# Near scores by one fp32 product a chunk in the edge attention, spread between the sum groups, and gathers without a pause on POOL

## The reference, cut to what matters

```python
h_all = einsum('nf,rof->rno', x, W).reshape(r, n, h, d)     # 8 relations, 8 heads of 32
h_src = h_all[edge_type, src]                               # one row an edge
h_dst = h_all[edge_type, dst]
scores = einsum('ehd,hd->eh', h_src, attn_src) + einsum('ehd,hd->eh', h_dst, attn_dst)
scores = where(scores > 0, scores, 0.2 * scores)
amax = maximum(segment_max(scores, dst), 0.0)
w = exp(scores - amax[dst])
w = w / (segment_sum(w, dst) + 1e-12)[dst]
out = segment_sum(h_src * w[..., None], dst)
```

## Time and profile before

| what | before |
|---|---|
| time, median of three runs | 4772.35 us |
| the three runs | 4758.54 to 4772.65 us |
| the profiled execution, its own time | 4762.77 us |
| its span on the core | 4761.1 us |
| mean granted clock of PE | 0.827 of 2.4 GHz |
| bytes moved by transfers | 387.91 MB, mean 81 GB/s |

### The profile page before, as it was taken

One profiled execution on the slowest core, in us unless ns is written; L12 is line 12 of the kernel. 1 busy time (PEld: TensorE's weight loads), 2 busy tenths in 40 slices (PEclk: granted clock), 3 DMA queues, 4 the chain that ended last, 5 costly groups with the idle time before them and its releaser, 6 DMA issues. The chain is left out here.

```text
span 4761.1 us, 55035 instructions
## 1 busy us (share of the span) xinstructions
PE 3172.2 (67%) x15106; PEld 2308.6 (48%) x15107; DVE 2073.8 (44%) x4472; ACT 620.2 (13%) x1234; POOL 1288.2 (27%) x2031
## 2 busy tenths in 40 slices
PE   1899799679846317999459512256556665637998
PEld 0666588568735316777334212144344444425555
DVE  6999501310143630000233374365666666732333
ACT  0111100100022102322112100000000000002222
POOL 2700100000010230000300002787878887500000
PEclk9999899889978658999769856577777777857999
DMA  3522244244300012112223103344444444200000
GB/s 105 214 96 96 97 124 131 62 124 124 96 10 0 0 59 76 48 48 84 65 91 150 52 0 57 96 124 116 118 114 125 124 121 119 83 31 20 14 13 27
DMA packets 315432, 387.91 MB, mean 81 GB/s; under 512 B 43120, under 2 KB 259521, under 8 KB 311873
## 3 DMA queue, kind: packets, MB, share of 16 engines
q1 hardware_dynamic: 240642, 222.05, 14.2%
q0 software_dynamic: 49040, 140.22, 10.5%
q10 hardware_dynamic: 25648, 24.42, 1.7%
HBM read 271.43 MB, written 115.17 MB: 81 GB/s over the span
## 5 line engine op out<-in xcount | busy, mean ns | idle before, releaser
L1987 POOL DMA_INDIRECT att_ring<-relation_rows,table_row x784 | 777.3, 991 | 119.9 <-issue 4.7
L2098 PE MATMUL att_acc<-att_ring,att_onehot 128*128 128x264 f32 x1568 | 487.7, 464 | 22.8 <-issue 21.6
L2098 PEld LDWEIGHTS att_acc<-att_ring,att_onehot 128*128 128x128 f32 x1568 | 345.0, 231 | 115.1 <-issue 52.6
L446 PE MATMUL counts_acc<-onehot_lo,onehot_key 128*128 128x400 bf16 x2000 | 362.5, 337 | 43.0 <-DVE onehot_key L428 43.0
L2061 PE MATMUL att_po<-att_near,att_onehotT 128*128 128x64 bf16 x2352 | 147.0, 204 | 315.0 <-issue 263.2
L425 DVE TENSOR_SCALAR onehot_lo<-node_ids,source_lo 128x800 bf16<-128x800 int16 x1000 | 350.4, 416 | 0.0
L446 PEld LDWEIGHTS counts_acc<-onehot_lo,onehot_key 128*128 128x128 bf16 x2000 | 267.9, 139 | 141.7 <-DVE onehot_key L428 82.7
L625 PE MATMUL agg_agg<-x_gnn,agg_slab 128*128 128x257 f32 x1250 | 277.5, 381 | 66.1 <-DMA agg_slab<-edge_counts 66.1
L625 PE MATMUL agg_agg<-xn,agg_slab 128*128 128x257 f32 x1250 | 278.6, 382 | 22.5 <-DMA agg_slab<-edge_counts 22.5
L625 PEld LDWEIGHTS agg_agg<-x_gnn,agg_slab 128*128 128x128 f32 x1250 | 237.9, 190 | 101.9 <-DMA agg_slab<-edge_counts 66.5
L2061 PEld LDWEIGHTS att_po<-att_near,att_onehotT 128*128 128x128 bf16 x2352 | 104.5, 103 | 351.7 <-issue 351.6
(11 more groups left out here) (397 smaller groups left out, 4542.5 us busy)
## 6 DMA issues: line engine op xcount, KB each, us to landing
agg_slab<-edge_counts SPq DMA_DIRECT2D x50, 1600.0 KB, 7.4
edge_counts<-counts_out SPq DMA_DIRECT2D x100, 400.0 KB, 2.4
relation_rows<-tab_out SPq DMA_DIRECT2D x25, 1056.0 KB, 4.0
att_targets<-targets SPq DMA_DIRECT2D x28, 896.0 KB
wide_w<-L_ffn_W ACTq DMA_DIRECT2D x14, 1024.0 KB, 6.9
att_ring<-relation_rows,table_row POOLq DMA_INDIRECT x784
expert_rows_in<-blank_rows POOLq DMA_DIRECT2D x34, 256.0 KB
expert_rows_out<-blank_rows POOLq DMA_DIRECT2D x33, 256.0 KB
```

Source lines behind the costliest of these rows:

```text
L446: mm = nc.tensor.matmul(acc[:, k, h, 0:HALF_LO], oh_key[:, k, :, j], oh_lo[:, k, j, h * HALF_LO:(h + 1) * HALF_LO], start=False, stop=Fals ...
L1987: nc.gpsimd.indirect_dma_start(slots(p)[:, j, :], None, rows_of, bass.IndirectOffsetOnAxis(ap=c.row[:, n:n + 1], axis=0)).then_inc(landed[ ...
L2098: mm = nc.tensor.matmul(acc[:, 0:RW], oh[:, j, :], slots(p)[:, j, :], start=j == 0, stop=False)
```

## The change

- The near scores stay fp32: one piece in place of three in `relation_tables`, its store and `attend`. PE makes one fp32 product a chunk (28 calls a part) in place of three bfloat16 ones.
- These products no longer stand in one block. Group 0 of part p+2 stands after `flip(p+1)` and ahead of the first sum group, group 1 after `to_column(p+1, 0)`, group 2 after `to_column(p+1, 1)`, and groups 3 to 6 where all stood.
- The transposed one-hot is fp32 and is made in two halves: one ahead of the first scan, one after the sum one-hots 5 and 6.
- POOL issues the gathers without the addition and its wait.
- The scores are no longer stored in `attend`; the branch for unsorted edges works them out anew.
- SP's part loads run three parts ahead.

```diff
@@ relation_tables, the drain @@
-                    link(nc.vector.tensor_copy(by_head(near[:, b, 0, :]), own))
-                    link(nc.vector.tensor_tensor(by_head(rest[:, b, :]), own, by_head(near[:, b, 0, :]), ALU.subtract))
-                    link(nc.vector.tensor_copy(near[:, b, 1, :], rest[:, b, :]))
-                    link(nc.vector.tensor_tensor(rest[:, b, :], rest[:, b, :], near[:, b, 1, :], ALU.subtract))
-                    nc.vector.tensor_copy(near[:, b, 2, :], rest[:, b, :]).then_inc(read_v, 1)
+                    nc.vector.tensor_copy(near[:, b, :].rearrange("p (h r) -> p r h", h=HD), own).then_inc(read_v, 1)
@@ attend @@
-        ohT = g.sb(ctx, f"{name}_onehotT", [P, PE_LEN], BF16)
-        near = g.sb(ctx, f"{name}_near", [P, 2, 3, sc], BF16)
+        ohT = g.sb(ctx, f"{name}_onehotT", [P, PE_LEN])
+        near = g.sb(ctx, f"{name}_near", [P, 2, sc])
@@ attend, POOL @@
-                    pl.wait_ge(paused, n + 1)
-                    nc.gpsimd.tensor_tensor(pause, pause, pause, ALU.add).then_inc(paused, 1)
@@ attend, SP @@
                     if p:
-                        sp.wait_ge(ohT_ready, p)
+                        sp.wait_ge(ohT_ready, 2 * p)
...
+                part_loads(2)
                 for p in range(NPART):
-                    if p + 2 < NPART:
-                        part_loads(p + 2)
+                    if p + 3 < NPART:
+                        part_loads(p + 3)
@@ attend, ACT @@
-                    act.wait_ge(st_ready, p + 1)
-                    act.dma_start(kept[p, :, :], st[:, p % 2, :, :, :].rearrange("p c h r -> p (c h r)")
-                                  ).then_inc(st_kept[p % 2], 16)
@@ attend, PE @@
+                def own_scores(p, *groups):
+                    if p >= NPART:
+                        return
+                    for q in groups:
+                        if q == 0:
+                            pe.wait_ge(near_in[p % 2], 16 * (p // 2 + 1))
+                            pe.wait_ge(ohT_ready, 2 * p + 1)
+                            if p:
+                                pe.wait_ge(own_ready, p)
+                        if q == half // MGRP:
+                            pe.wait_ge(ohT_ready, 2 * p + 2)
+                        for j in range(q * MGRP, (q + 1) * MGRP):
                             mm = nc.tensor.matmul(po[:, j // bank, j % bank * sc:(j % bank + 1) * sc],
+                                                  ohT[:, j * P:(j + 1) * P], near[:, p % 2, :], start=True, stop=True)
+                        if q == MG - 1:
+                            mm.then_inc(own_sum, 1)
...
                         flip(p + 1)
+                    own_scores(p + 2, 0)
                     of_this(p, 0)
...
                         to_column(p + 1, 0)
+                    own_scores(p + 2, 1)
                     of_this(p, 2)
...
                         to_column(p + 1, 1)
+                    own_scores(p + 2, 2)
                     of_this(p, 4)
                     if more:
                         flip_back(p + 1)
-                    if p + 2 < NPART:
-                        own_scores(p + 2)
+                    own_scores(p + 2, 3, 4, 5, 6)
                     of_this(p, 5)
@@ attend, DVE @@
-                    nc.vector.tensor_scalar(ohT, tb, lane_a[:, 0:1], None, ALU.is_equal).then_inc(ohT_ready, 1)
+                    part = slice(k * half * P, (k + 1) * half * P)
+                    nc.vector.tensor_scalar(ohT[:, part], tb[:, part], lane_a[:, 0:1], None, ALU.is_equal
+                                            ).then_inc(ohT_ready, 1)
...
-                    if p >= 2:
-                        v.wait_ge(st_kept[p % 2], 16 * (p // 2))
...
                     n = p + 1
+                    if n + 1 < NPART:
+                        targets_of_lanes(n + 1, 0)
                     if n < NPART:
                         v.wait_ge(turned, n + 1)
                         scan_runs(n, 0, ahead, pseq[0:PH, 0:2 * P])
                     onehots(p, 5)
                     onehots(p, 6)
+                    if n + 1 < NPART:
+                        targets_of_lanes(n + 1, 1)
...
-                    if n + 1 < NPART:
-                        targets_of_lanes(n + 1)
                     onehots(n, 1)
```

More of the change, by code:

```diff
@@ L1912, in _, with attend @@
                 link(nc.vector.tensor_copy(c.unsorted, first))
-def attend(g, name, c, gaps, table, near_rows, targets, sums, kept):
+def attend(g, name, c, gaps, table, near_rows, targets, sums):
     nc = g.nc
@@ L1946, in attend @@
         carry = g.sb(ctx, f"{name}_carry", [1, RW])
-        pause = g.sb(ctx, f"{name}_pause", [1, 1], I32)
-        paused = g.sem(f"{name}_paused")
         po = g.ps(ctx, f"{name}_po", [P, 4, MMN])
@@ L1960, in attend @@
         landed = [g.sem(f"{name}_landed{k}") for k in range(RING)]
-        st_kept, near_in = ([g.sem(f"{name}_{n}{k}") for k in range(2)] for n in ("scores_kept", "near_in"))
+        near_in = [g.sem(f"{name}_near_in{k}") for k in range(2)]
         (tb_in, chain_s, st_ready, turned, ends, row_out, into_in, col_out, scanned, back, less_ready, share_ready,
@@ L1979, in _ @@
             def _(pl):
-                nc.gpsimd.memset(pause, 0).then_inc(paused, 1)
                 for n in range(NC):
@@ L2012, in _ @@
                 sp.wait_ge(stored, 16 * NPART)
-                for k in range(2):
-                    sp.wait_ge(st_kept[k], 16 * (NPART // 2))
             @block.scalar
@@ L2112, in nothing @@
                     pass
-                own_scores(0)
+                own_scores(0, *range(MG))
                 for p in range(-1, NPART):
@@ L2260, in onehots @@
                         ALU.is_equal).then_inc(oh_ready, 1)
-                targets_of_lanes(0)
+                targets_of_lanes(0, 0)
+                targets_of_lanes(0, 1)
                 own_scores(0)
@@ L2762, in build_program @@
             g.end_of_stage()
-            attend(g, "att", c, gaps, table, dst_rows, targets, sums, kept)
+            attend(g, "att", c, gaps, table, dst_rows, targets, sums)
         g.end_of_stage()
@@ L2768, in build_program @@
             greatest = g.sb(own, "greatest", [P, NC, HD])
-            late_scores(g, c, kept, scores)
+            late_scores(g, c, table, dst_rows, scores)
             g.end_of_stage()
```

107 lines of the change are left out of this document (63 added, 44 removed).

## The result

The changed kernel takes 4742.2 us (median of 5 runs, 4739.9 to 4749.4) against 4770.2 for the kernel before in 5 runs: a ratio of 0.9956, interval 0.9941 to 0.9971. It is faster by 28 us, where 118 was forecast. The profiled execution took 4744.5 us, 18 less than the profiled one before.

The account below looks back on a forecast made before the run. POOL's gathers were taken as the pace for nine tenths, ring waits for the rest. 42 us (POOL's pace), 75 (ring waits) and 1 (tables' tail) made 118 off 4762.8: 4645 us, range 4575 to 4765.

Parts of the forecast that it names:

- POOL's pace: Gathers in `attend`: without the addition, POOL's floor falls from 1066 to 1024 us, 36.6 a part, 42 us less.
- The disturbance by the fp32 one-hot: Gathers beside DVE's transposed one-hot are stretched; with two fp32 halves this grows from 24 to 40 us.
- the 62 set beside it: By the skill page's lock rule, all of the fp32 one-hot's time would stall POOL: 62 us in place of 40.
- the hold-up: PE's short bfloat16 near products are held up while gathers run; DVE waits about 10.5 us a part for them.
- the 42 of this term: The gain from POOL's pace in `attend`: its floor of 1066 us becomes 1024.
- One bound: DVE's one-hot half in fp32, read from the sum groups' one-hot, 512 elements in 0.67 us: about 2 us.
- Ring waits, 75 us: POOL's waits for a free ring group in `attend` fall from 115 to 40 us; bounds 0 and 115.
- the hold-up stays and is only paid elsewhere: Rival: near products still held up beside gathers, ring waits stay 115, only POOL's 42 us won: 4720 us, chance 0.16.
- The sign that the prediction's last sentence names: In `attend`, DVE's wait moving to the row and column exchanges would show the forecast wrong; no size given.
- Slower: Rival: held-up near products stand ahead of the sum groups, 6.9 us a part more: 4893 or 4851 us, chance 0.13.
- the forecast's own mechanism: In `attend`, hold-up mostly gone and POOL the pace: 4645 us, own range 4565 to 4705, chance 0.62.

Follow-up runs that it names:

- e5: The changed kernel unaltered, on a chip without the hold-up: 4587.5 us, 0.9879 of the kernel before.
- e13: The kernel before without POOL's addition and its wait, transposed one-hot built on ACT in two passes, chip without the hold-up: 4548.6 us, 0.9799.
- e8: The kernel before with only POOL's small addition and its wait taken out, chip without the hold-up: 4569.3 us, 0.9839.
- e6: The changed kernel with POOL's small addition and its wait put back ahead of each gather, chip without the hold-up: 4648.3 us, 1.001.
- e3: The changed kernel with near products over 16 of 64 columns from part 2 on, chip with the hold-up: 4794.5 us, 1.002.
- e18: The changed kernel with 32 one-number copies a part added on ACT, chip with the hold-up: 4752.3 us, 0.999.
- e4: The kernel before with one bfloat16 piece of three multiplied for the near scores, chip with the hold-up: 4728.3 us, 0.988.
- e2: The changed kernel with 27 of 28 near products a part left out from the third part on, chip with the hold-up: 4721.9 us, 0.987.
- e1: The changed kernel with the gathers of parts 3 to 27 left out, chip with the hold-up: 4545.9 us, 0.950.
- e16: The kernel of e13 (no addition, one-hot on ACT) on a chip with the hold-up: 4851.5 us, 1.014 of the kernel before.
- e17: The changed kernel with gathers fetching rows of 132 floats in place of 264 from part 3 on, chip with the hold-up: 4750.3 us, 0.998.
- e15: The changed kernel with 32 one-number copies a part added on ACT, chip without the hold-up: 4591.4 us, 0.989.

## Why the prediction failed

**POOL's pace: right.** 1.25 us a gather, halves of 1.15 us, 1024 us for all gathers (1023 measured in e5, 6 of them ring waits), 36.6 us a part (36.6). The disturbance by the fp32 one-hot, 40 us, comes to 784 x (1001 - 956) ns = 35 (e5 against e13), and not to the 62 set beside it; against the old one-hot it is 19 us more, where I had 16 (e5 against e8). Only the start of this term was low: from the chip with the hold-up I read 1066 us for POOL with the addition, and e6 has 1083, mainly because I took all of the 115.5 us of the earlier trace rows for ring waits, while e6 has 13.3 us there with no wait for the ring among them. Where nothing else limits, the change gives 57 us for the 42 of this term. One bound was misread: 512 elements in 0.67 us make 2.3 us for a half, not 2; with 1.15 measured, nothing hung on it.

**Ring waits, 75 us: the step that failed.** They were to fall from 115 to 40 us and rose to 152. The term rested on the sentence that what falls is the hold-up, because fp32 sum groups are not held up beside gathers. As I now read the earlier trace rows, the sum groups ran free because they stood behind near products that had taken the hold-up on themselves. With near products that are issued within 4 us, the sum group behind them crawls. The hold-up takes whatever is issued, fp32 too and whatever its size (the sum groups above, e3), and on ACT too (e18). It goes by instructions rather than by work (e3, e4): some are let through at full speed, and then one per 0.7 or 1.4 us, 2.8 in the first fill. But with 108 fewer of them a part (e2) the starts crawl no longer and POOL still waits 126 us, so a count of instructions isn't the whole of it. The change takes away a third of the near products' instructions, and the loop of DVE and PE hardly gained by it: scores come 41.0 us apart between the second and the last but one, 41.8 before, where 33 are possible on such a chip without gathers (e1). POOL without waits went from 1066 to 780.0 + 221.8 = 1002 us, and since the loop sets the pace, most of that came back as waits: 64 won, 37 given back, 27 us off POOL's sum. The medians lie 28 us apart, the two profiled executions 18, so that the 27 meets the 28 is in part chance. e16 had still less of POOL's own work, and more waits and a slower loop. On the chips without the hold-up the 75 us did not exist: e6, with the addition, has no wait for the ring. So the term was wrong on either kind of chip.

**Rivals.** The nearest was "the hold-up stays and is only paid elsewhere", 4720 at 0.16: its mechanism is the one that the trace shows, paid at the sum groups and, in the first fill, at the exchanges (21.5 us at one row copy, 25.6 at the maxima). The sign that the prediction's last sentence names, DVE's wait moving to the exchanges, is a weak one: most of it stands on the chip without the hold-up too (e5). The rival held the ring waits at 115 and the pace's gain at 42; they came to 152 and 64. "Slower" did not come: in the steady parts the near groups ahead of the exchanges were not held up at all (1.5, 0.8 and 0.8 us, as in e5). That the time lies within the stated range, 4575 to 4765, is the rivals' doing, for the range took them in; the forecast's own mechanism, 4565 to 4705, didn't hold it.

**A sentence to take back.** I wrote that the rows don't bear out the rule of the Trainium skill's page "SBUF — State Buffer", section "Who interferes with whom", by which DMA never contends with a compute engine. The 2.6 against 20.7 us only showed that the hold-up goes with gathers. e17 (half the bytes, same hold-up) and ACT's copies, which use no DMA, agree with the rule: no run shows memory traffic to hold the engines up.

**What stays open** is what the engines wait for. It is shown that it hits PE and ACT alike, that it is gone without gathers (e1), that it outlasts them by 11 us after the first fill, and that it goes with the chip: no chip changed its kind between its runs, and the one chip without it that came up twice (e5 and e15) was without it both times.

Two plain explanations fall by the traces. The gathers' transfers are no slower on such a chip: their packets take 7.8 ms in sum (10.3% of 16 engines over 4743 us) against 8.0 in e5 (10.9% over 4585). Nor is it the clock: without gathers (e1) such a chip grants 0.81 in the stretch from 3300 to 3600 us, where with them it grants 0.70 and e5 0.78. Of the 155 us between the two kinds, 49 fall in the first fill alone (85.5 us from the first to the second score, 36.7 in e5).

One more difference lies in the traces: the changed kernel's trace of the first result holds 20,024 changes of semaphores, that of e5 31,567, of the same program; nearly all that are missing are the landings of gathers. It is the same for the kernel of e13 and e16: 32,056 on the chip without the hold-up, 18,952 on the one with it. So I take it that what is short is the way out for the records of the profile itself. That some 18 copies pass before the crawl looks as if each engine had a small store for them; that is a guess. The Trainium skill's page "NOTIFIC — the notification-queue block", section "Overflow: three behaviours, one of which stalls the engine", says that this path holds back its producers rather than losing a record inside; the crawl would agree, the 11,500 changes of semaphores that are missing would not. Its section "Constraints, capacities, measured rates" says that emitting an implicit record costs the engine nothing; if my reading holds, the 32 copies, 14 us where they take 3, disagree. No time here was taken without a record, so this is argued and not shown, and if it is so, the difference between the two kinds of chip may be one of the measurement and not of the kernel.

## What to carry to other kernels

Before a wait is charged to what runs beside it, look whether instructions of another engine, small and dependent on nothing, crawl in the same steps: if they do (e18), the limit is not in the engine whose wait you see. A wait for a free slot is a difference of two paces; shortening the work of the engine that waits makes it grow (e16) and may win nothing. And a gain by pace is read from the engine that sets it (POOL's sum moved with the whole time in e5, e6, e8 and e13 to within 5 us), while a gain by waits should get its own chance until what ends the waits is known; here two chips with the same program were 155 us apart.

## What the hardware showed beyond that

- The same program takes 4587.5 us on one chip and 4742.2 on another, at granted clocks of 0.831 and 0.818, nearly all of the difference in one stage, where POOL waits 152 us for the ring on the one and 6 on the other.
- An indirect gather of 128 rows takes 1.25 us from start to start for rows of 1056 and of 528 bytes alike.
- DVE's comparison that builds the one-hot costs POOL about half of its own time: removing 28 x 1.21 = 34 us of it (e8 to e13) made gathers 784 x 20 ns = 16 us shorter and the kernel 21 to 22 us faster (on other chips).
- A one-hot out of ACT, by a square and a cut at zero, took 2 x 3.28 us for 3584 elements and was hidden in full while POOL was the pace.
